# Row norms of k and q from products with two constant columns, in a one-core layer kernel

## What is computed

```
def _l2norm(x):
    return x * jax.lax.rsqrt(jnp.sum(x * x, -1, keepdims=True) + 1e-06)
...
q = _short_conv(x @ Wq, qc_w).reshape(b, l, NH, DK)
k = _short_conv(x @ Wk, kc_w).reshape(b, l, NH, DK)
...
q = _l2norm(q)
k = _l2norm(k)
```

## Time and profile before

| | |
|---|---|
| median of the timed executions | 1187.01 us |
| the profiled execution, its span | 1185.62 us, 1183.9 us |
| TensorE busy | 1046.3 us, 88% of the span |
| VectorE busy | 807.8 us, 68% |
| ScalarE busy | 546.1 us, 46% |
| GpSimd busy | 413.5 us, 35% |
| mean granted TensorE clock | 0.947 of full |

### The profile page before, as it was taken

One profiled execution on the slowest core, in us unless ns is written; L12 is line 12 of the kernel. 1 busy time (PEld: TensorE's weight loads), 2 busy tenths in 40 slices (PEclk: granted clock), 3 DMA queues, 4 the chain that ended last, 5 costly groups with the idle time before them and its releaser, 6 DMA issues.

```text
span 1183.9 us, 25577 instructions
## 1 busy us (share of the span) xinstructions
PE 1046.3 (88%) x10348; PEld 774.6 (65%) x10348; DVE 807.8 (68%) x1548; ACT 546.1 (46%) x965; POOL 413.5 (35%) x648
## 2 busy tenths in 40 slices
PE   3948899899989999899989999899989999897738
PEld 2833785588638885588637885488637885486427
DVE  6584468775887578775887578775887577753363
ACT  2254347443664348443564348443565348432421
POOL 7118300960058200950058200951058200950000
PEclk9988899999999999999999999999999999995759
DMA  5140103020220104020220104020230204020000
GB/s 159 20 106 3 36 19 90 19 53 2 66 61 15 41 19 107 2 54 2 64 63 13 43 19 103 5 53 2 56 70 7 49 1 100 9 53 1 1 0 18
DMA packets 82932, 47.44 MB, mean 40 GB/s; under 512 B 58496, under 2 KB 76416, under 8 KB 82816
## 3 DMA queue, kind: packets, MB, share of 16 engines
q1 hardware_dynamic: 82816, 45.82, 16.7%
HBM read 31.12 MB, written 14.68 MB: 39 GB/s over the span
## 4 chain that ended last, share of the span: by engine, by line
PE 64%; DVE 18%; ACT 10%; POOL 3%; issue 3%; DMA 2%; SPq 1%; DVEq 0%; ACTq 0%; POOLq 0%
PE psum L788 14%; PE psum L790 12%; PE psum L789 12%; PE psum L819 4%; DVE arena L1637 3%; PE psum L981 3%; PE psum L966 3%; PE psum L1000 3%; PE psum L1005 2%; ACT arena L586 2%; PE psum L1160 2%; DVE arena L1639 2%; POOL l_prod L524 1%; POOL arena L528 1%; PE psum L956 1%
## 5 line engine op out<-in xcount | busy, mean ns | idle before, releaser
L524 POOL TENSOR_TENSOR l_prod<-arena 64x30 f32<-64x30 f32 (+14 forms) x240 | 149.6, 623 | 553.6 <-DMA arena<-l_dram 535.4
L582 ACT ACTIVATE h_f<-psum,b_col 128x512 f32<-128x512 f32 x128 | 88.0, 688 | 209.8 <-PE psum L790 207.4
L528 POOL TENSOR_TENSOR arena<-arena,l_prod 64x30 f32<-64x30 f32 (+14 forms) x240 | 158.7, 661 | 18.8
L1087 PE MATMUL psum<-v_shift,fir_w 128*32 128x512 f32 x1152 | 140.6, 618 | 12.2 <-DVE wo_lo L1249 12.2
L788 PE MATMUL psum<-w_hi,h_hi 128*128 128x256 f32 x512 | 149.9, 293 | 0.1
L790 PE MATMUL psum<-w_hi,h_lo 128*128 128x256 f32 x512 | 143.5, 280 | 0.0
L789 PE MATMUL psum<-w_lo,h_hi 128*128 128x256 f32 x512 | 143.5, 280 | 0.0
L1359 DVE CAST h_hi<-h_f 128x512 fp32r<-128x512 f32 x128 | 62.4, 488 | 91.8 <-PE psum L790 45.4
L788 PE MATMUL psum<-xt_hi,w_hi 128*128 128x512 f32 x256 | 109.3, 427 | 16.1 <-DVE b_half L1484 7.5
L1386 DVE SCALAR_TENSOR_TENSOR conv_acc<-psum,conv_col,conv_acc 128x511 f32<-128x511 f32 x144 | 106.9, 748 | 15.1 <-ACT conv_acc L607 11.4
L789 PE MATMUL psum<-xt_lo,w_hi 128*128 128x512 f32 x256 | 103.4, 404 | 0.0
(11 more groups left out here) (231 smaller groups left out, 2181.9 us busy)
## 6 DMA issues: line engine op xcount, KB each, us to landing
x_in<-in_L_attn_x SPq DMA_DIRECT2D x8, 512.0 KB, 3.9
v_dram<-v_fm SPq DMA_DIRECT2D x16, 256.0 KB, 3.0
v_shift<-v_dram SPq DMA_DIRECT2D x16, 256.0 KB, 3.5
out<-x_tok SPq DMA_DIRECT2D x8, 512.0 KB, 2.9
v_shift<-v_dram SPq DMA_DIRECT2D x16, 255.5 KB, 4.4
v_shift<-v_dram SPq DMA_DIRECT2D x16, 255.0 KB, 5.1
v_shift<-v_dram SPq DMA_DIRECT2D x16, 254.5 KB, 5.7
arena<-in_L_ffn_w SPq DMA_DIRECT2D x2, 1024.0 KB, 7.1
```

What stands on the lines that cost most here:

```text
L524: pool.tensor_tensor(prod, l_inv[:, k + 1:, k:k + 1].broadcast_to(shape), l_inv[:, k:k + 1, 0:k].broadcast_to(shape), ALU.mult).then_inc(i ...
L528: pool.tensor_tensor(l_inv[:, k + 1:, 0:k], l_inv[:, k + 1:, 0:k], prod, ALU.add).then_inc(inverted, 1)
L582: act.activation(h_f[:, m % 2, :], bank, ACT.Gelu, bias=b1_col[:, m:m + 1]).then_inc(read, 1)
L1087: last = pe.matmul(fir[p][0][col:col + 32, :], fir_w[:, group, n - 1 if n else TAPG, :], v_shift[:, group, at_t:at_t + T], start=(n < 2), ...
```

## The change

q is no longer turned. ScalarE squares k and q where the convolution left them, with channels on partitions and out of SBUF, each 128x512 tile on its own. A constant `pair_sel` of two columns has ones in rows 0 to 63 of the first and 64 to 127 of the second. For each of four blocks of 128 tokens and each of the two tiles TensorE multiplies the block of squares (as the stationary operand, 128x128) with these two columns: eight products give 128 tokens x 16 units in PSUM. For k they follow `k_products` and land in the bank of `beta_t`, whose reader is released only after them; for q they stand where the turn was. VectorE adds 1e-6 straight out of PSUM; both reductions go. All is float32.

```
-        q_sq = at_flat[:, 0:TILES * C].rearrange("p (u d) -> p u d", u=UNITS)
+        k_sq = sq[:, :, :]
+        q_sq = at_flat[:, 0:HALVES * T].rearrange("p (h t) -> p h t", h=HALVES)
...
-        Q = [("q_t", (3, 5))]
+        Q = [("q_sum", (3,))]
...
+                make(pool.memset(pair_sel[part, half:half + 1], 1.0))
...
-                    for t in range(2):
-                        bank, _ = arrive(act, at, "k_t", t)
-                        act.activation(sq[:, t, :], bank, ACT.Square).then_inc(kq_squared, 1)
+                    for h in range(HALVES):
+                        act.wait_ge(silu_made, 6 * j + 3 + h)
+                        act.activation(k_sq[:, h, :], qk_fm[:, h, 0, :], ACT.Square).then_inc(kq_squared, 1)
...
+                    for h in range(HALVES):
+                        act.wait_ge(silu_made, 6 * j + 5 + h)
+                        act.activation(q_sq[:, h, :], qk_fm[:, h, 1, :], ACT.Square).then_inc(kq_squared, 1)
                     for h in range(2):
                         out_of(at, "fir", h, f_fm[:, h, :])
-                    for t in range(2):
-                        bank, read = arrive(act, at, "q_t", t)
-                        act.activation(at_flat[:, 512 * t:512 * t + 512], bank, ACT.Square).then_inc(kq_squared, 1)
...
+            def square_sums(cols, squares):
+                for t in range(TILES):
+                    for h in range(HALVES):
+                        first = HEADS * t + 2 * h
+                        last = pe.matmul(cols[:, first:first + 2], squares[:, h, P * t:P * t + P], pair_sel[:, :],
+                                         start=True, stop=True)
+                return last
+
+            def k_sums(at):
+                bank, full = where(at, "beta_t")
+                pe.wait_ge(kq_squared, 4 * at.j + 2)
+                square_sums(bank[:, TILES * 32:TILES * 32 + UNITS], k_sq).then_inc(full, 1)
...
                     k_products(at)
+                    k_sums(at)
                     projection(at, "q", 1, 1)
...
-                    pe.wait_ge(silu_made, 6 * j + 6)
-                    to_tok(at, "q_t", lambda h: qk_fm[:, h, 1, :])
+                    q_sums(at)
...
                 def k_rows():
                     bank, read = arrive(dve, at, "beta_t")
+                    dve.tensor_scalar(nrm[:, 0, :], bank[:, TILES * 32:TILES * 32 + UNITS], 1e-6, None, ALU.add).then_inc(nrm_made, 1)
                     link(dve.tensor_copy(rows_tok[:, 1, :].rearrange("p (t h) -> p t h", t=TILES),
...
-                    dve.wait_ge(kq_squared, 4 * j + 2)
-                    link(dve.tensor_reduce(rows_tok[:, 0, :], sq_u, AX.X, ALU.add))
-                    dve.tensor_scalar(nrm[:, 0, :], rows_tok[:, 0, :], 1e-6, None, ALU.add).then_inc(nrm_made, 1)
...
-                    dve.wait_ge(kq_squared, 4 * j + 4)
-                    link(dve.tensor_reduce(rows_tok[:, 2, :], q_sq, AX.X, ALU.add))
-                    dve.tensor_scalar(nrm[:, 1, :], rows_tok[:, 2, :], 1e-6, None, ALU.add).then_inc(qnrm_made, 1)
+                    bank, read = arrive(dve, at, "q_sum")
+                    dve.tensor_scalar(nrm[:, 1, :], bank[:, 0:UNITS], 1e-6, None, ALU.add).then_inc(qnrm_made, 1)
```

More of the change, by code:

```diff
@@ L122, in macaron_kernel @@
         beta_fm = sb("beta_fm", [32, T])
+        pair_sel = sb("pair_sel", [P, 2])
         rows_tok = sb("rows_tok", [P, 3, UNITS])
@@ L320, in macaron_kernel @@
         T_LOADS = CPT + 2 * (CPT - 1)
-        DVE_STEPS = {"head": 43, "body": 70, "last": 65, "tail": 32}
-        CONST_MADE, C_LOADED, SETUP_DVE = 60, 57, 36
+        DVE_STEPS = {"head": 41, "body": 68, "last": 63, "tail": 32}
+        CONST_MADE, C_LOADED, SETUP_DVE = 63, 57, 36
         ZEROED, IDENT_MADE = 5, 7
@@ L469, in _ @@
             for t, v in ((low_strict[:, :], 1.0), (up_incl[:, :], 1.0), (eye32[:, :], 0.0), (x_t[:, :, :], 0.0),
-                         (stat_sel, 0.0), (mean_sel, 0.0), (head_mask, 0.0), (v_shift[:, :, :], 0.0),
+                         (stat_sel, 0.0), (mean_sel, 0.0), (head_mask, 0.0), (pair_sel[:, :], 0.0), (v_shift[:, :, :], 0.0),
                          (ms_tok[:, :, :], 0.0), (mx_tok[:, :, :], 0.0)):
@@ L735, in one_pass @@
                     silu(5)
+                    for h in range(HALVES):
+                        act.wait_ge(silu_made, 6 * j + 5 + h)
+                        act.activation(q_sq[:, h, :], qk_fm[:, h, 1, :], ACT.Square).then_inc(kq_squared, 1)
                     for h in range(2):
                         out_of(at, "fir", h, f_fm[:, h, :])
-                    for t in range(2):
-                        bank, read = arrive(act, at, "q_t", t)
-                        act.activation(at_flat[:, 512 * t:512 * t + 512], bank, ACT.Square).then_inc(kq_squared, 1)
-                        act.wait_ge(kq_squared, 4 * j + 3 + t)
-                        act.sem_inc(read, 1)
                 if at.back:
@@ L1029, in beta_turn, with q_sums @@
                 for t in range(TILES):
-                    last = pe.transpose(bank[:, 32 * t:32 * t + 32], beta_fm[:, P * t:P * t + P], ident[0:32, 0:32])
-                last.then_inc(full, 1)
+                    pe.transpose(bank[:, 32 * t:32 * t + 32], beta_fm[:, P * t:P * t + P], ident[0:32, 0:32])
+            def square_sums(cols, squares):
[9 more added lines that the diff above has]
+                square_sums(bank[:, TILES * 32:TILES * 32 + UNITS], k_sq).then_inc(full, 1)
+            def q_sums(at):
+                bank, full = claim(pe, at, "q_sum")
+                pe.wait_ge(kq_squared, 4 * at.j + 4)
+                square_sums(bank[:, 0:UNITS], q_sq).then_inc(full, 1)
             def k_products(at):
@@ L1559, in q_rows @@
                 def q_rows():
-                    dve.wait_ge(kq_squared, 4 * j + 4)
-                    link(dve.tensor_reduce(rows_tok[:, 2, :], q_sq, AX.X, ALU.add))
-                    dve.tensor_scalar(nrm[:, 1, :], rows_tok[:, 2, :], 1e-6, None, ALU.add).then_inc(qnrm_made, 1)
+                    bank, read = arrive(dve, at, "q_sum")
+                    dve.tensor_scalar(nrm[:, 1, :], bank[:, 0:UNITS], 1e-6, None, ALU.add).then_inc(qnrm_made, 1)
+                    dve.wait_ge(qnrm_made, j + 1)
+                    dve.sem_inc(read, 1)
                 def q_inverse():
```

## The result

The changed kernel takes 1196.25 us (median of 4 executions, 1194.43 to 1199.35) where the kernel before took 1186.9 beside it: a ratio of 1.0083, 95% interval 1.0058 to 1.0109. It is 9 us slower; 1188.0 was forecast, and 1196.0 was the end of the range. The profiled execution took 1194.43 us, its span 1192.7, so the sum of the prediction (1186.6 for a profiled execution) is missed by 7.8 us.

A forecast was written before the change was run, and what follows sets the result against it. TensorE carries 64% of the chain, but both edits lie on the path. Passes 6.0, clock -9.5, falls at the sums +1.3, head +3.2 give +1.0 us: 1186.6 profiled, 1188.0 timed, range 1184.5 to 1196.

The forecast's parts named there:

- The sums: k in a body pass: 16 matmuls, 0.111 us each, 1.78 us; k's root starts 1.15 us later.
- The head: Head pass: sums take 3.3 us at the low clock, root +3.0 us; +3.2 us taken, bounds 1.3 and 5.
- q: Mixture to norm in a body pass: reduction goes, ScalarE's square hides most; 0.30 us saved, bounds 0 and 0.32.
- The clock behind the turn: Turn of the mixture: wait falls from 2.43 to 1.23 us, all or nearly all six clock falls go, -9.5 us.
- A wait of 1.23 lies below the 1.85 at which the clock held: Ahead of the turn of the mixture: the first body waited 1.85 us and kept clock 1.00, so 1.23 should too.
- The falls at the sums: Clock falls where two-column sums leave the array nearly empty: +1.3 us in all, bounds 0 and 3.5.
- I reckon them as the pass shown: Seven fronts with a back beside them taken as alike: each 0.85 us longer, seven 6.0 us.
- the logits' wait: TensorE's 0.95 us wait ahead of the logits' products; with the GELU 1.15 later, it covers 1.78 us of sums.
- the first rival: Slower: clock falls in the bodies as before, fewer than four of six go; 1194 to 1197.5 us, chance 24%.

The follow-up runs named there:

- 60 idle instructions at the covered place: Changed kernel plus 60 no-effect TensorE instructions ahead of the head's FIR filters, where TensorE waits 12.5 us: 1186.70 us, ratio 1.0007 to the kernel before.
- q alone: Kernel before with only the edits for q, k's norm as before: 1175.16 us, ratio 0.9920.
- added work: Kernel before plus five matmuls with overwritten results ahead of the turn of the mixture, in seven passes: 1179.36 us, ratio 0.9953.
- the control: Kernel before, otherwise unchanged, plus 60 no-effect TensorE instructions ahead of the head's FIR filters: ratio 1.0001.
- the edits of k alone: Kernel before with only the edits for k; q turned, squared out of PSUM and reduced as before: 1204.00 us, ratio 1.0147.
- the sums ahead: Changed kernel with the sums of k ahead of k's products instead of behind them: 1184.73 us, ratio 0.9999 to the kernel before.

## Why the prediction was wrong

*The sums.* Right: 16 weight loads in 1.86 us (0.111 each was forecast), the root 4.44 us after the start of k's turn (597.42 to 601.86) where it was 3.28: 1.16 later, forecast 1.15.

*The head.* Right: its root comes 7.20 us after the turn instead of 4.10, 3.1 later where 3.0 was forecast; the first merge is at 136.17 (136.6). But the term hangs on the low clock there. With 60 idle instructions at the covered place, the head is the same up to this point, and yet in that execution its sums took 1.95 us instead of 3.57, and the first merge came at 135.2.

*q.* Right: from the last piece of the mixture to the reduction behind it 2.48 us where it was 2.80, 0.3 less, and the reduction starts 0.03 after the square ends:

```profile
488.45 1.35 DVE L1657 TENSOR_TENSOR arena<-arena 128x1024 f32<-128x1024 f32 x1
...
489.84 1.06 ACT L746 ACTIVATE arena<-arena 128x1024 f32<-128x1024 f32 x1 [4.74 <-DVE arena L1657]
...
490.93 1.22 DVE L1662 TENSOR_REDUCE oss<-arena 128x16 f32<-128x1024 f32 x1 [1.04 <-ACT arena L746]
```

*The clock behind the turn.* Right in the six passes: in all ten kernels with a shorter wait the clock held behind the turn from the second pass to the last, and that work ahead of the wait does it is shown from two sides (q alone, and added work). The reason given, "A wait of 1.23 lies below the 1.85 at which the clock held", is not enough: the clock fell behind 1.52 us in the first pass, a fall that was not foreseen and is most of its 2.2 us, and held behind 2.76 us in the control and behind 2.2 to 2.6 us in four passes with the edits of k alone, where it had fallen earlier in the pass. The length of the wait alone does not tell. The falls at the sums, +1.3 us, cost nothing that the passes without a stall show: behind the sums of the fourth pass the clock was 0.50 from 601.8 to 605.2, and the pass took 132.45 us where 132.7 was forecast.

*The step that failed* is the one that reckons seven passes alike: "I reckon them as the pass shown", with the logits' wait of 0.95 us and the GELU as cover for TensorE. The place of a piece of code in the program is not the same in every pass. The change moved the block ends by 48 instructions a pass and lengthened the run of small matmuls; in the profiled execution three stalls of 2.2 to 2.4 us took the place of two of 1.0 and 1.65. The trace of before showed one at 728.17, and I had taken the 0.4 us around it for the price of a clock of 0.50 alone. The same 0.4 us misled me about its price in the new kernel. Before, k's root did not wait for TensorE, and the logits' wait, which is gone in that pass, took up 0.95 of the 1.65 us; the turn of the mixture came 0.4 us later than in the pass ahead. In the changed kernel the root waits for the sums that queue behind the stall, and the turn came 91.0 us after the merge in the third pass (stall of 2.44 us) and 88.3 in the fourth. Without the stalls the forecast stands within 2 us, 1.0007 against 1.0008. The miss of 7.8 us closes in the profiled executions: the passes are 11.0 us above their forecast, the head 0.5 below it, the part behind the last merge, which the change does not touch, 1.4 shorter than before (120.8 instead of 122.2 us), and 1.3 had been allowed for the clock at the sums, which makes 7.8. That the first rival's range, 1194 to 1197.5, holds the result is no merit of it: all six falls that it kept are gone.

The profile names no releaser for the stalls, but the traces of the 13 kernels tell what TensorE waits for. They have 34 idle times of its matmuls of over 0.15 us that are put down to "issue", of which 28 are over 0.6 us. All 34 stand at the same place of a block: where the loads, products and semaphore instructions of TensorE's program, counted from its first, are 191 over a multiple of 256. And each ends 1.2 to 1.6 us after an instruction packet has landed. So these are waits for the next 256 instructions. A block end among small matmuls does not suffice, though: at 105, 107 and 114 there was none in some passes. At 105 in the first pass of the changed kernel the packet started at 194.39 and landed at 195.63, ahead of the block end at 197.59; in the three passes with a stall it started 0.1 to 0.3 us ahead of the stall. What decides when a packet is fetched stays open.

## What to carry to other kernels

Where a program of many passes is unrolled, look at a short stretch in all of its passes, not in one: a wait for "issue" in the midst of a run of small matmuls, whose place drifts from pass to pass, moves with every instruction added or removed anywhere ahead of it. Before such a change is judged, shift it by some idle instructions at a covered place; here that was worth 9 us, the whole loss. With TensorE's instructions counted modulo 256 the places can be worked out ahead. And a short wait of TensorE that the clock answers with a fall can be worth filling, with useful work or without.

## What the runs showed of the hardware

- In 128 matmuls of 32 columns (1.29 us) TensorE stalls for 1.6 to 2.8 us at a place given by the count of its instructions modulo 256, from matmul 98 on (0.7 and 0.2 us at 95 and 101 with the sums ahead of them); two instructions a matmul. It goes on 1.2 to 1.6 us after a packet of 16 KB on the instruction queue has landed; such a packet takes about 1.0 us.
- A count on a semaphore in TensorE's program costs about 0.15 us: 122 of them ahead of the first matmul let it start at 21.48 us, 128 at 22.39, where it starts at 12.5 without. 60 of them hid in that wait.
- The clock fell behind a wait of 1.52 us and held behind one of 2.76 us over the same turns, in a pass in which it had fallen 25 us earlier.
- 16 products of 2 or of 64 columns, each behind a load of 128x128 weights of its own, take 1.95 or 2.00 us, and the loads 1.86 in both.
- One kernel spreads over up to 12 us from one execution to the next (1178.14 to 1190.15 with the sums ahead), so a profiled execution has to be held against its own time and not the median.
